# First attention: the scores of a pair of heads as passes on two row halves, one bank for q, k and v

## The reference, cut to what matters

```python
def _L0_xattn_ref(x, latents, ...):          # x: the context, latents: the running x
    DIM, HEADS, DIM_HEAD = 256, 16, 64
    xn, latn = layernorm(x), layernorm(latents)
    q = latn @ Wq                            # 256 queries, 1024 wide
    k, v = split(concat([xn, latn]) @ Wkv)   # 512 keys
    weight = softmax((q * scale) @ (k * scale).T)   # per head, scale = 64 ** -0.25
    return (weight @ v) @ Wo
```

## Time and profile before

| | us |
|---|---|
| median of three runs | 1675.24 (1675.08 to 1678.4) |
| the profiled execution's own time | 1679.34 |
| its span | 1677.6 |
| PE busy | 1476.6 (88%) |
| DVE busy | 1020.5 (61%) |
| ACT busy | 879.3 (52%) |
| POOL busy | 458.2 (27%) |

### The profile page before, as it was taken

How to read it: one execution, slowest core, us unless ns; L and a number is a source line. 1 busy time by engine, 2 the same in 40 slices (tenths; PEclk the granted TensorE clock), 3 DMA queues, 4 the chain that set the end, 5 groups by cost and what they waited for, 6 DMA issues and landing times. The chain is left out here.

```text
span 1677.6 us, 28402 instructions
## 1 busy us (share of the span) xinstructions
PE 1476.6 (88%) x9884; PEld 1198.7 (71%) x9884; DVE 1020.5 (61%) x2142; ACT 879.3 (52%) x2200; POOL 458.2 (27%) x395
## 2 busy tenths in 40 slices
PE   3899999999999999959799998499999629999995
PEld 3678777777777778747698896365655518888885
DVE  5877777777777876755321114477778654444452
ACT  2676767675767777735211113366666214445442
POOL 5110101010101010033200015232322015777774
PEclk9999999999999999977899999599999659999998
DMA  3300000000000000012279993100000223445442
GB/s 113 110 14 1 14 1 14 1 14 2 14 1 14 1 1 1 1 38 93 112 253 312 318 329 69 29 14 7 14 1 2 92 78 101 120 120 126 122 115 34
DMA packets 72255, 118.17 MB, mean 70 GB/s; under 512 B 6864, under 2 KB 52944, under 8 KB 72112
## 3 DMA queue, kind: packets, MB, share of 16 engines
q1 hardware_dynamic: 61408, 99.66, 18.0%
q0 software_dynamic: 10704, 16.65, 4.9%
HBM read 97.68 MB, written 18.61 MB: 69 GB/s over the span
## 5 line engine op out<-in xcount | busy, mean ns | idle before, releaser
L435 ACT ACTIVATE a_p<-a_s,a_negmax 128x512 f32<-128x512 f32 x256 | 176.0, 688 | 156.9 <-DVE a_negmax L603 115.3
L603 DVE TENSOR_REDUCE a_negmax<-a_s 128x1 f32<-128x512 f32 x256 | 176.2, 688 | 47.9 <-PE a_s L298 37.9
L207 POOL TENSOR_TENSOR a_o_l<-a_o,a_o_h 128x256 fp32r<-128x256 f32 x64 | 47.0, 735 | 559.7 <-ACT a_o_h L460 559.7
L1491 ACT ACTIVATE h_probs<-h_scores,h_negmax 128x256 f32<-128x256 f32 x256 | 117.8, 473 | 83.4 <-DVE h_negmax L1658 83.4
L307 PEld LDWEIGHTS a_t<-ident,a_p 128*128 128x128 f32 x1024 | 120.6, 140 | 52.9 <-issue 18.1
L307 PE MATMUL a_t<-ident,a_p 128*128 128x128 f32 x1024 | 156.9, 276 | 0.6 <-DVE a_pT L618 0.6
L1903 POOL TENSOR_TENSOR n_w_l<-n_raw,n_w_h 128x768 fp32r<-128x768 f32 x64 | 118.3, 1849 | 75.2 <-ACT n_w_h L1946 75.2
L597 DVE TENSOR_TENSOR a_k_hl<-a_k_p,a_k_hl 64x512 fp32r<-64x512 f32 x128 | 88.2, 689 | 71.3 <-ACT a_k_hl L418 70.2
L325 PE MATMUL a_out_p<-a_pT,a_v 128*64 128x256 f32 x1024 | 124.6, 385 | 0.0
L297 PE MATMUL a_s<-a_k_hl,a_q_hh 128*128 128x512 f32 x256 | 108.2, 423 | 9.1 <-ACT a_p L435 7.1
L1658 DVE TENSOR_REDUCE h_negmax<-h_scores 128x4 f32<-128x1024 f32 x64 | 78.1, 1221 | 49.6 <-PE h_scores L1585 49.6
(11 more groups left out here) (325 smaller groups left out, 4290.2 us busy)
## 6 DMA issues: line engine op xcount, KB each, us to landing
e_w_in<-in_L_ffn_gate_up_proj SPq DMA_DIRECT2D x31, 1024.0 KB
n_raw<-in_L_ffn_w SPq DMA_DIRECT2D x64, 384.0 KB, 3.0
e_w_out<-in_L_ffn_down_proj SPq DMA_DIRECT2D x31, 512.0 KB
rows_in<-a_zeros SPq DMA_DIRECT2D x1, 3968.0 KB, 15.6
e_rows<-rows_in SPq DMA_DIRECT2D x31, 128.0 KB, 5.1
rows_out<-e_result POOLq DMA_DIRECT2D x31, 128.0 KB, 4.6
x<-in_x SPq DMA_DIRECT2D x8, 256.0 KB, 2.9
a_ctx_in<-in_ctx SPq DMA_DIRECT2D x8, 256.0 KB, 3.1
```

Of the source, the lines that this page charges most:

```text
L435: act.activation(probs[j][:, :], scores[j % 2][:, :], ACT.Exp, bias=negmax[:, j:j + 1], accum_out=total[:, r % 2, j % 2, j // 2:j // 2 + 1 ...
L603: dve.tensor_reduce(negmax[:, j:j + 1], scores[j % 2][:, :], AX.X, ALU.max, negate=True).then_inc(max_set, 1)
L1491: ins = act.activation(probs[s % 4][:, j, :], scores[s % 2][:, j // 2, j % 2, :], ACT.Exp, bias=negmax[:, s % 4, j:j + 1], accum_out=total ...
```

## The change

The scores of both heads of a pair are now made together, for 128 queries at a time. For each of the three passes, two matmuls of 64 rows follow each other, one head on the upper row half and one on the lower, each into a bank of its own; a score tile has two banks, and there are two tiles. q and k have plain tiles of 128 partitions, a high part and a rest, so each is written once. The separate banks of q, k and v are gone: `proj` takes all of them in turn, with waits between. v's copy is made by DVE and not by ACT. One maximum covers both heads (1024 wide, two results).

```diff
-        scores = [psum(f"a_s{i}", [P, N]) for i in range(2)]
-        out_p, k_p, v_p = psum("a_out_p", [P, 2, S]), psum("a_k_p", [P, N]), psum("a_v_p", [P, 2, 2 * P])
-        q_p = psum("a_q_p", [P, N])
+        scores = [psum(f"a_s{i}", [P, 2, N]) for i in range(2)]
+        out_p, proj = psum("a_out_p", [P, 2, S]), psum("a_proj", [P, N])
...
-                    pe.matmul(scores[j % 2][:, :], q_hh[r % 2][:, h, rows], k_hl[r % 2][h][:, :], start=True, stop=False)
-                    pe.matmul(scores[j % 2][:, :], q_l[r % 2][:, h, rows], k_hl[r % 2][h][:, :],
-                              start=False, stop=True).then_inc(s_done, 1)
+                    for i, (s, m) in enumerate(((q_h, k_h), (q_h, k_l), (q_l, k_h))):
+                        for h, rows in enumerate(halves):
+                            ins = pe.matmul(scores[half][:, h, :], s[r % 2][rows, at], m[r % 2][rows, :],
+                                            start=(i == 0), stop=(i == 2))
+                    ins.then_inc(s_done, 1)
...
                         score(b, r, 0)
+                        pe.wait_ge(kl_set, PAIRS * b + r + 1)
+                        if r == 2:
+                            wait(pe, added, b)
+                        if r in (4, 5) and last < 2:
+                            pe.wait_ge(filled, KC * (b + 1) + r - 3)
+                        project_v(b, r // 2, r % 2, bp, first and bp == 0)
                         if prev:
+                            turn(*prev, 1)
+                        if nxt:
+                            pe.wait_ge(v_set, PAIRS * b + r + 1)
+                            project_q(*nxt, first and bp == 0)
+                        score(b, r, 1)
+                        turn(b, r, 0)
+                        if nxt:
+                            project_k(*nxt)
+                        if prev:
+                            attend(*prev)
+                        if nxt:
+                            if (r == 1 and not first) or (r in (3, 4) and last < 2):
+                                pe.wait_ge(kl_set, PAIRS * b + r + 2)
+                            if r == 1 and not first:
+                                project_out(b - 1)
+                            if r in (3, 4) and last < 2:
+                                turn_inputs(b + 1, r - 3)
...
                     def between(r, j):
-                        if last < 2 and 4 * r + j < PARTS:
-                            prepare(b + 1, 4 * r + j)
+                        for part in range(8 * r + 2 * j, 8 * r + 2 * j + 2):
+                            if last < 2 and part < PARTS:
+                                prepare(b + 1, part)
...
+                        if r == 2 and not first:
+                            add(b - 1)
+                        if r in (4, 5) and last < 2:
+                            fill(b + 1, r - 4)
                         maximum(b, r, 0)
+                        set_v(b, r // 2, r % 2)
+                        if prev:
+                            set_odd(*prev, 1)
+                            invert(*prev)
+                        between(r, 0)
+                        if done:
+                            set_out(*done)
+                        if nxt:
+                            low_q(*nxt[:2])
+                        between(r, 1)
+                        maximum(b, r, 1)
+                        set_odd(b, r, 0)
+                        between(r, 2)
+                        if nxt:
+                            low_k(*nxt[:2])
+                        between(r, 3)
```

More of the change, by code:

```diff
@@ L225, in step @@
                     for r in range(PAIRS):
[L226 to L231, removed]
+                        done = before_that(b, r, first)
+                        if done:
+                            low_o(*done)
+                        if r in (4, 5) and last < 2:
+                            low_kv(b + 1, 1 - bp, r - 4)
                 pool.memset(g.ident[:, :], 0.0).then_inc(ident_set, 1)
@@ L326, in attend @@
                                             probsT[r % 2][h][:, c, :], start=(c == 0), stop=(c == NC - 1))
+                    pe.wait_ge(spread_set, s + 1)
+                    for half in range(2):
+                        ins = pe.transpose(out_p[:, 1, half * P:(half + 1) * P], inverses[r % 2][:, half, :, :], g.ident[:, :])
                     ins.then_inc(o_done, 1)
@@ L407, in set_q @@
                     act.wait_ge(q_done, s + 1)
-                    wait(act, s_done, 4 * s - 4)
-                    for h in range(2):
-                        for half in halves:
-                            ins = act.activation(q_hh[r % 2][half, h, :], q_p[halves[h], 0:S], ACT.Copy, scale=QSCALE)
-                    ins.then_inc(qh_set, 1)
-                def set_k(b, r):
-                    act.wait_ge(k_done, PAIRS * b + r + 1)
-                    for h, half in enumerate(halves):
-                        ins = act.activation(k_hl[r % 2][h][half, :], k_p[half, :], ACT.Copy)
-                    ins.then_inc(kh_set, 1)
@@ L421, in set_v @@
[L421 to L436 removed]
+                    wait(act, s_done, 2 * s - 2)
@@ L463, in step @@
                     for r in range(PAIRS):
-                        prev, nxt = before(b, r, first), after(b, r, bp, last)
-                        exponent(b, r, 0)
+                        prev, nxt, done = before(b, r, first), after(b, r, bp, last), before_that(b, r, first)
+                        exponent(b, r, 0, 0)
+                        exponent(b, r, 0, 1)
                         if prev:
-                            set_even(*prev, 2)
-                        if r == 6 and last < 2:
-                            high_kv(b + 1, 1 - bp, 1)
+                            set_even(*prev, 1)
+                            spread(*prev)
@@ L470, in step @@
+                        if nxt:
+                            set_q(*nxt[:2])
+                        set_even(b, r, 0)
+                        if done:
+                            high_o(*done)
+                        if r in (4, 5) and last < 2:
+                            high_kv(b + 1, 1 - bp, r - 4)
+                        exponent(b, r, 1, 0)
                         if nxt:
                             set_k(*nxt[:2])
-                        exponent(b, r, 1)
-                        if prev:
-                            spread(*prev)
@@ L594, in low_k @@
                 def low_k(b, r):
                     dve.wait_ge(kh_set, PAIRS * b + r + 1)
[L596 to L604 removed]
+                    dve.tensor_tensor(k_l[r % 2][:, :], proj[:, :], k_h[r % 2][:, :], ALU.subtract).then_inc(kl_set, 1)
@@ new lines, in set_v, with maximum @@
+                def set_v(b, group, half):
+                    m = PAIRS * b + 2 * group + half
+                    dve.wait_ge(v_done, m + 1)
+                    wait(dve, o_done, m - half - 2)
+                    dve.tensor_copy(v[group % 2][:, 2 * half:2 * half + 2, :], v_p[:, :, :]).then_inc(v_set, 1)
+                def maximum(b, r, half):
+                    dve.wait_ge(s_done, 2 * (PAIRS * b + r) + half + 1)
+                    dve.tensor_reduce(negmax[:, half, :], scores[half][:, :, :], AX.X, ALU.max, negate=True).then_inc(max_set, 1)
```

211 lines of the change are left out of this document (70 added, 141 removed).

## The result

The changed kernel takes 1727.28 us (median of four runs, 1719.73 to 1737.71) against 1675.16 for the kernel before: 1.0314 times the time before [1.0287, 1.0342]. It is slower by 52 us. The forecast was slower by 15; 1727 lies above the range's end of 1710.

A forecast was written before the change was run, and what follows sets the result against it. PE was taken to bound the kernel, with DVE close behind. Six middle batches +15, the first +1.5 but starting 1.5 earlier, the last +0.8: +15 on 1675.2 gave 1690 us, range 1658 to 1710.

The forecast's parts named there:

- The 2.2 of waiting before the output projection: End of step r = 1: PE, free at 10.3, waits 2.2 us for k's rest on DVE, ending at 12.4.
- the 0.18 behind v's copy: Every step: q's projection waits 0.18 us until DVE has copied v out of the common bank.
- the earlier start of 1.5: First batch: starts about 1.5 us earlier, as v's two projections no longer stand ahead of the first score.
- ACT's relief: ACT: fewer writes of q and k and no v copy, worth nothing because ACT has room already.
- Rivals 1 and 2: Whole kernel: waits in r = 0 to 2 half as long, 1660, chance 0.24; no change within 3.4 us, 0.08.
- Rivals 3 and 4: Score block: weight loads wait for their row group, 1725, chance 0.05; row halves run one after another, 1765, 0.03.
- the size of the score block: Each score block on PE: three pairs at 0.23 plus 0.20 for entering and leaving the divided array, 0.89 us.
- saving of 0.08 a step: PE's score work: two blocks take 1.78 us where four scores took 1.86, 5 us over 64 steps.
- plain step: Step without preparation: PE's work of 9.23 us plus 0.18 of waiting, 9.4.
- the same +1.5 as the others: First batch: the stalls of r = 0 and 1 but no output projection, 1.5 us longer.
- 15 + 1.5 - 1.5 + 0.8: First attention: six middle batches +15, first batch +1.5 and starting 1.5 earlier, last batch +0.8 us.
- The 5.7 us of waits a batch: Kernel before, middle batches: 81.1 us of PE work in 86.8, the other 5.7 waits where PE stands behind DVE.

The follow-up runs named there:

- e1: Changed kernel with one part of the preparation per place instead of two; 1680.66 us, 1.0039 times the kernel before.
- e2: Changed kernel with each score block as four matmuls of 128 rows, not six of 64 (part of the computation left out); 1714.78 us, 1.0234 times the kernel before.
- e6: Changed kernel with GpSimd's split of the output weights moved to r = 2 and 3 of the first batch; 1720.52 us, 1.0289 times the kernel before.

## Why the prediction was wrong

**Right.** The direction and its mechanism. The forecast put the loss into the steps r = 0 and 1, behind two parts of preparation a place, with `attend` and the output projection queued behind PE's waits, and e1 shows that it is there. Lengths at full clock against the forecast, in us: r = 0 12.0 (11.9), r = 1 18.6 (18.1), r = 2 10.2 (10.5), r = 3 10.3 (9.8), r = 4 10.6 (10.3), r = 5 10.1 (9.9), r = 6 and 7 9.85 (9.4). The 2.2 of waiting before the output projection was measured as 2.17, the 0.18 behind v's copy as 0.16, the earlier start of 1.5 as 1.7. ACT's relief of 141 us bought nothing that can be seen, as said; no run takes it by itself. Rivals 1 and 2 (heavy steps hide more, no change) fall with r = 0 at 12.0. Rivals 3 and 4 fall with pairs 0.23 apart: at that spacing neither does a weight load hold up its pair nor one half the other. The Trainium skill, TensorE: Matmul & The Clock Gate, section Part 3: Packing small matmuls, says in one sentence that loads overlap with matmuls in flight only when the row group differs, and in another that the background weight buffer will do as well. The trace goes against the first: each half gets new weights for every pass, and the loads do not show in the 0.23. The second would allow it; which of the two buffers a load went to, no run here shows.

**The step that failed: the size of the score block, 0.20 for going into the divided array and out.** Each block costs 0.40 (e2). I took 0.20 from the second attention, from the block's first start to the transposes behind it, and with it only the part that lies inside the block. The pass ahead of that block stood in the same rows and I did not read it: it holds 0.21 (1149.14 to 1149.35) where such a pass takes 0.12, 0.09 more. The same is seen at the new block: 0.09 are paid by the f32r pass before it (at the second block of a step), 0.10 by the first pair, 0.10 by the last, and 0.10 by the first f32r pass behind it (at the first block, which v's passes follow). The first block stands behind float32 transposes and the second ahead of them, so no one block shows all four shares; 0.40 is the mean of the two in a step. From first start to transposes the block is 0.90, as forecast with 0.89, and looks right if one reads only that far. With it the saving of 0.08 a step on PE became a loss of 0.3, and the plain step 9.85. Clean batches take 91.5 instead of 89.3, 13.2 us in six, but not all of that is the block's. By e2's measure (1.2 a batch for 0.32 a step) the missing 0.40 a step is worth some 1.5 of the 2.2 a batch, an estimate, or 9 us in six. Another 0.4 a batch is a slip of the sum: laid end to end, the prediction's own plain step is 5.86 + 1.48 + 2.15 = 9.49, and 9.4 went into the five light steps. The Trainium skill, TensorEngine Tiling (Array Packing), section Key Properties, says that a change of tiling mode drains the array; the trace agrees, with 0.40 a block.

**Two terms were put at nothing.**
- The clock. Behind waits of PE of 1.5 to 2.3 us it drops to 1.2 GHz for 3.4 us at a time, seven times in the middle batches, where before it never did. Six of the waits are the new ones in r = 0 and 1; the seventh (2.1, at the end of an r = 7) stood in the kernel before too, with 1.9 and a clock of 1.00. By the excess of those steps over the same step at full clock (r = 1: 3.2, 3.0, 1.7, 1.6; r = 0: 2.1) it costs 11.6 us in that execution. I had counted a wait as its own length only.
- The first batch. The forecast gave it the same +1.5 as the others. DVE's preparation now lies at r = 0, where GpSimd still splits the output weights. r = 0 takes 16.9, PE stands still for 9.3, and 10.2 us at half clock begin within that wait. The batch is 9.3 longer, 7.8 more than forecast; e6 gives 6.5 of it back. The meeting was there to be read in the kernel before, where two such operations were held, the longer one here (0.17 alone):

```profile
42.53 2.26 DVE L512 TENSOR_SCALAR a_var<-a_mv 128x4 f32<-128x4 f32 x1
```

In the changed kernel four are held, 7.7 us together. The Trainium skill, SBUF — State Buffer, section Who interferes with whom, has the rule: a VectorE instruction with two inputs in SBUF contends with a GpSimd instruction that reads SBUF, one in a mode of two ports contends with GpSimd too, and one with at most one input in SBUF outside those modes does not. The trace agrees: the two TENSOR_TENSOR were held for 2.18 and 2.30, and the copy out of PSUM at 46.01 took its usual 0.68 under GpSimd's cast. In which mode the held TENSOR_SCALAR ran, no run here shows.

**The account.** The forecast's terms sum to 15.8 (15 + 1.5 - 1.5 + 0.8), the profiled executions differ by 58.4, so 42.6 were missed. The six middle batches have 29.9 of it: 13.2 in their clean length, 11.6 by the clock, and 5.1 at r = 0 and 2 of the inner batches (0.2 to 0.5 each) and in one r = 7 (2.1, which was there before as well). The first batch has 7.8. The last, with the end of the stage, has 6.6: 3.0 in its first seven steps, and 3.7 behind them, where PE waits for DVE 1.73 and the clock falls twice. There `attend` takes 3.27 where the same 16 matmuls took 1.95 in the kernel before:

```profile
775.78 3.27 PE L324 MATMUL a_out_p<-a_pT,a_v 128*64 128x256 f32 x16 [1.73 <-DVE a_o L603]
```

The earlier start and the stages behind give back 1.7 more than forecast. The profiled execution of the changed kernel was the slowest of the four, 10.4 above the median, where that of the kernel before was 4.2 above, so a part of the 58 belongs to that execution. The clock does differ between executions: its mean over the whole program was 0.936 in this one, and 0.945, 0.939 and 0.945 in those of 1719.73, 1729.79 and 1724.76 us. How often it fell in the first attention of those three is open, and with it how much of the 52 us of the medians is the clock's.

One reading of the kernel before was off as well. The 5.7 us of waits a batch were put down to DVE. Of the 20.8 us of waits that the profile counts for PE in the six batches, 10.5 are for DVE; the others are for GpSimd (3.3), for ACT (2.4), or without a cause that it shows (4.6).

## What to carry to other kernels

Take the price of an array mode from a place where the neighbours are of the same kind as in your kernel, and measure from the pass before the block to the second pass behind it: 0.2 inside the block and 0.2 outside made a gain of 0.08 a step a loss of 0.3. When work of a helper engine is packed closer, look at what it now stands beside (another engine's phase, the end of a burst), since waits of 1.5 us and more were followed by a slower clock here as well. The best thing found was not in the change: a reading of who waits for which of two queued operations, and an exchange of the two, gave 1.0%, and a second one about 0.5% more.

## What the hardware showed that was not expected

- Matmuls on the two row halves, in pairs with fresh weights each: 0.235 a pair of 512 columns, the same as one pass at full height. A block of three pairs pays 0.40 for its edges, the mean of the two blocks of a step.
- Tiny operations of DVE in SBUF (128x4) lasted until GpSimd's running operation ended, 1.0 to 2.3 us for 0.16.
- A wait of about 2 us of PE, in a stage where it is busy 94% of the time, was followed by 3.4 us at 1.2 GHz in some batches, and in others not: batches 1 and 6 have the same wait, at a clock of 1.00.
